# Third graph layer: the vector engine's steps of the last passage put behind the pair product, and fewer, wider writes on GpSimd

## What is computed

```python
log_ij = _logmap(x[:, None, :], x[None, :, :], c)      # every pair of nodes
agg = jnp.einsum('ij,ijc->ic', adj / deg, log_ij)
transformed = agg @ weight + bias
return _expmap(origin, transformed, c)                 # tanh of the row's length, times the row
...
# the layer after it (index 3)
support = layernorm_relu(x) @ weight3                  # then a rank-weighted sum over the neighbours
```

## Time and profile before

| | us |
|---|---|
| three runs | 1113.17, 1117.30, 1118.21 |
| median | 1117.3 |
| the profiled execution | 1117.34 |
| its span | 1115.6 |
| third layer, unit 0's pair product to the last one's | 580.1 to 1003.9 |
| the last passage's steps in it | 814.4 to 982 |

### The profile page before, as it was taken

One profiled execution on the slowest core, in us unless ns is written; L12 is line 12 of the kernel. 1 busy time (PEld: TensorE's weight loads), 2 busy tenths in 40 slices (PEclk: granted clock), 3 DMA queues, 4 the chain that ended last, 5 costly groups with the idle time before them and its releaser, 6 DMA issues.

```text
span 1115.6 us, 14859 instructions
## 1 busy us (share of the span) xinstructions
PE 1038.4 (93%) x5404; PEld 457.0 (41%) x5404; DVE 865.2 (78%) x1011; ACT 757.6 (68%) x803; POOL 272.7 (24%) x145
## 2 busy tenths in 40 slices
PE   4899999999669999999998998999999998989998
PEld 1233333336643333333333443444544454436544
DVE  6999989996476666688668977877779887778781
ACT  2454554543355666686688889888888888777782
POOL 3179300000010000004005364444343433330010
PEclk9999999998879999999999999999999999989999
DMA  7999999991008888787764444555545545446451
GB/s 264 409 390 351 355 355 317 356 363 56 1 4 298 279 287 283 260 277 272 256 198 140 145 132 158 181 176 170 183 151 189 161 160 189 132 145 223 133 180 39
DMA packets 98438, 240.42 MB, mean 215 GB/s; under 512 B 16449, under 2 KB 47169, under 8 KB 81985
## 3 DMA queue, kind: packets, MB, share of 16 engines
q1 hardware_dynamic: 89152, 222.72, 58.1%
q10 hardware_dynamic: 9216, 16.78, 3.9%
HBM read 221.65 MB, written 17.83 MB: 215 GB/s over the span
## 4 chain that ended last, share of the span: by engine, by line
PE 49%; issue 22%; POOL 13%; DVE 9%; ACT 5%; DMA 1%; SPq 1%; POOLq 0%; DVEq 0%; ACTq 0%
PE PS L555 35%; POOL ring L533 10%; PE PS L701 5%; PE PS L702 5%; POOL H L533 2%; DVE TB L1445 1%; DMA ring<-in_adj_t 1%; ACT work L1105 1%; PE PS L567 1%; DVE work L1894 1%; PE PS L589 1%; PE PS L579 1%; DVE work L1440 1%; PE PS L831 1%; ACT work L1008 1%
## 5 line engine op out<-in xcount | busy, mean ns | idle before, releaser
L1571 DVE TENSOR_TENSOR work<-work,ring 128x1024 f32<-128x1024 f32 x128 | 151.1, 1223 | 78.7 <-ACT work L1105 78.7
L1042 ACT ACTIVATE work<-PS 128x1024 uint8<-128x1024 f32 x128 | 124.1, 1020 | 120.3 <-PE PS L555 120.3
L1105 ACT ACTIVATE work<-PS,att_sc 128x1024 f32<-128x1024 f32 x128 | 147.5, 1201 | 80.3 <-PE PS L702 72.7
L555 PE MATMUL PS<-ring,work 128*65 128x256 f32 (+1 forms) x612 | 194.1, 466 | 2.2 <-DVE work L1922 1.2
L533 POOL TENSOR_TENSOR ring<-work,ring 128x1024 f32<-128x1024 f32 (+1 forms) x57 | 134.0, 2352 | 245.7 <-DVE work L1894 245.6
L555 PE MATMUL PS<-work 128*64 128x512 f32 (+3 forms) x800 | 153.6, 524 | 1.1 <-ACT work L1168 1.0
L1888 DVE SCALAR_TENSOR_TENSOR work<-PS,work 128x1024 f32<-128x1024 f32 x72 | 85.8, 1192 | 56.4 <-PE PS L555 49.9
L555 PEld LDWEIGHTS PS<-ring,work 128*65 128x65 f32 x612 | 83.5, 140 | 91.8 <-issue 66.9
L701 PE MATMUL PS<-work 128*128 128x512 f16 x256 | 98.8, 386 | 4.2 <-DVE work L1394 2.5
L1174 ACT ACTIVATE work<-work 128x1024 f32<-128x1024 f32 x72 | 74.2, 1031 | 37.2 <-DVE work L1882 37.2
L702 PE MATMUL PS<-work 128*128 128x512 f16 x256 | 98.2, 383 | 0.0
(11 more groups left out here) (248 smaller groups left out, 1488.9 us busy)
## 6 DMA issues: line engine op xcount, KB each, us to landing
ring<-in_adj_t SPq DMA_DIRECT2D x96, 1024.0 KB, 5.2
ring<-in_adj_t SPq DMA_DIRECT2D x107, 512.0 KB, 3.8
work<-in_adj_t SPq DMA_DIRECT2D x32, 1024.0 KB, 7.6
codes<-work ACTq DMA_DIRECT2D x64, 256.0 KB, 6.6
ring<-codes SPq DMA_DIRECT2D x64, 256.0 KB, 3.8
H<-in_adj_t SPq DMA_DIRECT2D x25, 512.0 KB, 3.8
X<-in_x SPq DMA_DIRECT2D x2, 512.0 KB, 5.2
out_x<-X SPq DMA_DIRECT2D x1, 512.0 KB, 3.8
```

The lines of the kernel that those rows point to most:

```text
L555: return mm(out_ap, lhsT, rhs, start=starts, stop=True, skip_group_check=True)
L1042: nc.scalar.activation(made[:, k, u * UNIT:(u + 1) * UNIT], PS[:, (4 + 2 * u) * BANK:(6 + 2 * u) * BANK], ACT.Relu).then_inc(sem("codes_ma ...
L1105: nc.scalar.activation(att[:, u, :], PS[:, (4 + 2 * u) * BANK:(6 + 2 * u) * BANK], ACT.Sigmoid, bias=att_sc[:, 2:3], scale=att_sc[:, 1:2]) ...
L1571: V.tensor_tensor(prob[:, m % 4, :], att[:, u, :], ring[:, s % RING, u * UNIT:(u + 1) * UNIT], ALU.mult)\
```

## The change

Three things are altered.

1. In DVE's loop `last_passage2(n)` and the early `near2_out` stand behind `pair2(n)`, not ahead of it.
2. The steps stand in other turns, in smaller parts, up to turn 70. PE's and ACT's tables follow: `to_last(0)` and `weighted_last(0)` move from 51 and 52 to 57 and 58, `to_tangent(1)` and `weighted(1)` from 57 and 58 to 59 and 60.
3. In POOL's `aux_nodes` two writes of 128 x 48 become one of 128 x 96, three times per call.

```diff
@@ POOL, aux_nodes
                 for k in range(3):
                     link(nc.gpsimd.tensor_copy(ALn[:, :, 3 * k:3 * k + 3], ...))
-                    for d in range(2):
-                        link(nc.gpsimd.tensor_copy(ARn[:, :, d, k:9:3], tpart[k][:, :].unsqueeze(2).broadcast_to([P, TG, 3])))
+                    link(nc.gpsimd.tensor_copy(ARn[:, :, :, k:9:3], tpart[k][:, :].unsqueeze(2).unsqueeze(3).broadcast_to([P, TG, 2, 3])))
@@ DVE, last_passage2 (turn: steps)
-40: tangent_dot(0), tangent_scale(0)
+39: tangent_dot(0)   40: tangent_scale(0)
 41: tangent_own(0), tangent_sum(0)   44: length(0)
-45: tanh_num(0, 0, 5)
+45: tanh_num(0, 0, 2)   46: tanh_num(0, 2, 5)
-46: length_root(0)   47: tanh_den(0), tanh_end(0)
+47: length_root(0)   48: tanh_den(0)   49: tanh_end(0)
-48: step_v(0), step_x(0)   49: mean3(0), centre3(0)
+50: step_v(0)   51: step_x(0)   52: mean3(0)   53: centre3(0)
-50: spread3(0)   51: feats3(0)   53: rest_a(0)   54: rest_b(0)
+54: spread3(0)   56: feats3(0)   59: rest_a(0)   60: rest_b(0)
-56: tangent_dot(1), tangent_scale(1)   57: tangent_own(1), tangent_sum(1)
+55: tangent_dot(1)   57: tangent_scale(1)   58: tangent_own(1), tangent_sum(1)
-60: length(1)   61: tanh_num(1, 0, 5)   62: length_root(1)
+62: length(1)   63: tanh_num(1, 0, 5)   64: length_root(1)
-63: tanh_den(1), tanh_end(1)   66: step_v(1), step_x(1)
+65: tanh_den(1)   66: tanh_end(1)   67: step_v(1)   68: step_x(1)
-67: mean3(1), centre3(1)
+69: mean3(1)   70: centre3(1)
@@ DVE, the loop over units
                 second_half2(n)
-                last_passage2(n)
-                if n - 2 in EARLY:
-                    near2_out(n - 2)
                 if n == NU - 1:
                     power(0)
                 pair2(n)
+                if n - 2 in EARLY:
+                    near2_out(n - 2)
+                last_passage2(n)
```

More of the change, by code:

```diff
@@ L79 @@
 COPIES = (2, 4, 7)
-VISITS = {38: ("agg2_copied", 2), 41: ("turned_out", 1), 42: ("z_out", 1), 51: ("turned_out", 2), 52: ("z_out", 2),
-          54: ("agg2_copied", 4), 57: ("turned_out", 3), 58: ("z_out", 3)}
+VISITS = {38: ("agg2_copied", 2), 42: ("turned_out", 1), 43: ("z_out", 1), 54: ("agg2_copied", 4),
+          57: ("turned_out", 2), 58: ("z_out", 2), 59: ("turned_out", 3), 60: ("z_out", 3)}
 CAUGHT = 16
@@ L875, in last_passage2 @@
                     nodes2(0)
-                if n == 41:
+                if n == 42:
                     to_tangent(0)
-                if n == 42:
+                if n == 43:
                     weighted(0)
[L880 to L883, removed]
                 if n == 54:
@@ L886, in last_passage2 @@
                 if n == 57:
+                    to_last(0)
+                if n == 58:
+                    weighted_last(0)
+                if n == 59:
                     to_tangent(1)
-                if n == 58:
+                if n == 60:
                     weighted(1)
@@ L1228, in last_passage2 @@
                     nodes2_out(0)
-                if n == 42:
+                if n == 43:
                     turned_out(0, 1)
-                if n == 43:
+                if n == 44:
                     z_out(0, 1)
@@ L1235, in last_passage2 @@
                     root_part("v_root", "v_norm2", 0, 0)
-                if n == 50:
+                if n == 54:
                     ln_square(0)
-                if n == 51:
+                if n == 55:
                     root_part("ln_sd", "ln_var", 3 * G, 0)
-                if n == 52:
+                    nodes2_out(1)
+                if n == 58:
                     turned_out(0, 2)
-                if n == 53:
+                if n == 59:
                     z_out(0, 2, W_SCALE)
                     part_a(0, 2)
-                if n == 54:
+                if n == 60:
+                    turned_out(1, 3)
                     part_b(0)
[L1247 to L1251, removed]
+                if n == 61:
                     z_out(1, 3)
-                if n == 60:
+                if n == 62:
                     v_square(1, 3)
-                if n == 61:
+                if n == 63:
                     root_part("v_root", "v_norm2", 1, 1)
@@ L1816, in last_passage2 @@
                     coefficients()
+                if n == 39:
+                    tangent_dot(0)
                 if n == 40:
-                    tangent_dot(0)
                     tangent_scale(0)
@@ L1825, in last_passage2 @@
                 if n == 45:
-                    tanh_num(0, 0, 5)
+                    tanh_num(0, 0, 2)
                 if n == 46:
+                    tanh_num(0, 2, 5)
+                if n == 47:
                     length_root(0)
-                if n == 47:
+                if n == 48:
                     tanh_den(0)
+                if n == 49:
                     tanh_end(0)
-                if n == 48:
+                if n == 50:
                     step_v(0)
+                if n == 51:
                     step_x(0)
-                if n == 49:
+                if n == 52:
                     mean3(0)
+                if n == 53:
                     centre3(0)
-                if n == 50:
+                if n == 54:
                     spread3(0)
-                if n == 51:
+                if n == 55:
+                    tangent_dot(1)
+                if n == 56:
                     feats3(0)
[L1842 to L1847, removed]
+                if n == 57:
                     tangent_scale(1)
-                if n == 57:
+                if n == 58:
                     tangent_own(1)
                     tangent_sum(1)
+                if n == 59:
+                    rest_a(0)
                 if n == 60:
+                    rest_b(0)
+                if n == 62:
                     length(1)
-                if n == 61:
+                if n == 63:
                     tanh_num(1, 0, 5)
-                if n == 62:
+                if n == 64:
                     length_root(1)
-                if n == 63:
+                if n == 65:
                     tanh_den(1)
+                if n == 66:
                     tanh_end(1)
-                if n == 66:
+                if n == 67:
                     step_v(1)
+                if n == 68:
                     step_x(1)
-                if n == 67:
+                if n == 69:
                     mean3(1)
+                if n == 70:
                     centre3(1)
```

## The result

The changed kernel takes 1138.8 us (median of four runs, 1136.4 to 1141.4), the kernel before 1116.2 us (1113.2 to 1118.2). The ratio is 1.020, with a 95% interval of 1.018 to 1.023: slower by 22.5 us, where 1135 us was forecast.

What follows compares the result with a forecast made beforehand. PE was taken to set the period, 5.86 us per pair product, with DVE having 1.35 us of slack. Terms 11.6 + 2.5 + 3.3 + 1.8 - 1.0 = +18.2 us on 1117.34 gave 1135 us, range 1110 to 1146.

Steps and rivals of the forecast that it cites:

- The mechanism: Behind the pair product, a step's second DVE operation waits for POOL's near product, 2.3 us; single-operation steps cost nothing.
- the unseen order: A DVE operation with two SBUF operands coming second to POOL: bounds 0 and 2.37 us, taken as 2.3.
- Rivals 1, 2 and 3: Only one-operand operations wait (1126, 0.13); no step waits for POOL (1110 to 1112); POOL waits each time; last two together 0.25.
- Rival 2: No step waits for POOL, each part fits DVE's slack: faster, 1110 to 1112 us; 0.25 together with the third rival.
- 58 to 62: Turns 58 to 61 and the transposes of turn 62: these come later despite moved visits, lower clock stays; +2.5 us.
- the middle: Turns 40 to 57: PE loses the DVE lag beyond 1.55 us, 12.7 us, less 1.1 of small waits; net +11.6.
- the slack: DVE's waits for PE ahead of far2_out and sum2 in a turn without steps: 1.35 us per turn.
- Rival 4: Turns 45 to 49: idle times of some 1.9 us lower the clock, up to 6 us more, 1141; chance within the forecast's 0.62.
- 62 to 67: Turns 62 to 67: lag from steps costs PE, less 1.2 us of small waits; about +3.3 us; turn 68's wait remains.
- near_out(69): After turn 71: near2_out(69) behind power(0) and the pair product delays PE's sum; +1.8 us, 0 at least.
- `near2_out(17)`: Moved behind the pair product it costs nothing, since PE waits for turn 20's pair product behind it anyway.
- POOL's writes: At aux_nodes(1): merged writes shorten PE's wait of 1.28 us; -1.0 us, bounds 0 and -1.28.

Runs made afterwards that it cites:

- ten steps behind: The changed kernel with its steps ahead of the pair product again, except ten one-operation steps left behind it: 1110.9 us, ratio 0.994 to the kernel before.
- `near_out` alone: The kernel before with only the early near2_out(17) and near2_out(69) moved behind power(0) and the pair product: 1120.2 us, ratio 1.0025.

## Why the prediction was right

**The mechanism** was that a step's second operation waits for POOL's near product. It is shown twice: in the rows (2.35 us for 0.17, in all 19 steps of several operations) and by moving POOL's start alone, which takes back 18 to 20 us. The value taken for the unseen order, 2.3 us, was measured at 2.2 of excess. The Trainium skill (SBUF — State Buffer, "Who interferes with whom") states both orders of this exclusion; the trace now agrees for both. The same section of the Trainium skill says that a reduction never contends on this chip; the trace agrees (0.68 us at 847.98). At 607.90 POOL's row starts 0.10 us before that of `rest2`, right at the end of POOL's near product; that POOL came second there is inferred from its standing still. Rivals 1, 2 and 3 fall: two-operand operations wait, steps of several operations do too, and DVE isn't let through first. Rival 2's time, 1110 to 1112, would not have come even without the conflict: that kernel (the changed one, POOL waiting) has a ratio of 1.004.

That the total came so close, 1135 for 1138.8, is partly luck: the turns 58 to 62 were put 2 us too high, the middle 1.7 and the end 3.3 us too low.

**The middle, 39 to 58:** +11.6 forecast, +13.3 measured. The size was nearly right, the place where PE feels it was not. I followed only the transposes' wait for the pair product. PE's larger waits are for `far2_out` and `near2_out`, which I had left out of the slack. The sum came out because DVE's period sets the time, whichever wait shows it: from the pair product of turn 44 to that of turn 50 DVE is busy for 43.6 of 44.5 us, where it was for 34.2 of 35.8 before. The pair products there are 6.8 to 8.1 us apart. The sum had no term for two things. One is PE's waits for ACT's copies at the visits (4.9 us, 1.1 before); these are in turns 43 and 58, where the turn behind a visit waits for its copy; `to_tangent(0)` and `weighted(0)` had moved too, from turns 41 and 42 to 42 and 43. The other is the clock. PE's idle time grew by 10.3 us where the forecast had 11.6, and the clock added some 3: it was half for 3.4 us twice, behind a wait of 2.26 us in turn 43 and one of 2.55 us in turn 46.

```profile
835.12 1.32 PE L830 MATMUL PS<-ident,work 128*128 128x128 f32 x8 [2.26 <-ACT TA L1007]
...
836.23 5.09 PE L554 MATMUL PS<-ring,work 128*65 128x512 f32 x12
...
859.12 5.32 PE L554 MATMUL PS<-H,work 128*65 128x512 f32 x12 [2.55 <-DVE work L1929]
```

Rival 4 had the clock, but over five turns in a row with small waits (45 to 49); from 863.1 us on it stayed up through the rest of them.

**58 to 62:** +2.5 forecast, +0.5 measured. This is the term that was sized wrongly. Followed, the transposes of turn 62 came 4.4 us later and the lower clock stayed. In the profile PE's waits there are 1.46 and 0.80 us, where it had 2.71 before, and the transposes of pair 61 take 1.09 us: the clock stayed up (1.00, before 0.93). That the moved visits filled PE better than I gave them credit for is my reading; no run separates it.

**62 to 67:** +3.3 forecast, +3.8 measured, but not from the waits forecast alone. The largest is 2.50 us, ahead of the scores of unit 67 (999.68), for `sum2` (1895). The wait of 2.94 us ahead of the transposes in turn 68, which was to remain, is 1.10 us now, and the stage 67 to 71 is 0.7 us shorter. The two stages together: +3.3 forecast, +3.1 measured. The sum left out turns 65 and 69, whose units are half as wide; their second operations wait 1.1 and 0.6 us.

**near_out(69):** the wait was right to 0.1 us (+1.8), the term was too small. The lower clock behind this wait adds 1.5 us, which the sum had at nothing; alone the edit costs 2.9 us (1.5 to 4.2). In the profile of the kernel after, a further 1.6 us go between turn 71 and the transposes at 1074: the clock is half for 3.4 us, from 1037.2 on. That is no consequence of the late `near2_out`. The profiles of six kernels with it ahead have the same stretch, the kernel with the wider writes alone among them, and there the stage behind unit 71 takes 113.9 us where the profile of the kernel before has 112.3. `near2_out(17)` cost nothing, as forecast.

**POOL's writes:** PE's wait fell from 1.28 to 0.54 us, 0.74 for a forecast 1.0. The third write is 0.92 us and the last operation of the call 1.24, since both still meet DVE's operations. From unit 0 to unit 39 the profiles of the seven kernels with the wider writes take 226.4 to 227.7 us, mean 226.9, those of the five without 227.5 to 228.4, mean 227.9: the 1.0 us of the forecast.

**Where the gain sits:** the forecast said that a better place could win little in the middle and most of it in turns 62 and 68. With the new turns and the steps ahead, 39 to 58 gains 2.6 us. 58 to 71 gains 5.3 us in the profiles, but 1.5 of it come back behind unit 71, and other profiles with the old order there have 71.3 to 75.8 us. The gain of the whole, by the ratio, is 3.8 us (2.0 to 5.6), within the 7.8 at most that rival 2 counted.

## What to carry to other kernels

Before small work is put into an engine's gap, ask what its neighbour does in that gap: DVE's slack behind the pair product was real, but it was POOL's time at the port. What reads one operand from PSUM can run there: `sum2` at 792.20 takes its 1.22 us beside POOL. Where DVE and POOL alternate, put chains of dependent DVE operations in POOL's idle time; a single operation can go right behind the one that starts POOL, since it gets ahead. When a producer moves within its turn, move the consumers' visits with it, and leave whatever others wait for (`near2_out`, `far2_out`) ahead of the filler.

## What was unexpected of the hardware

- A DVE operation of eight elements per partition waits as long as one of 512: 2.35 us (1747), and 2.73 us in all for 128x512 (1739). What it pays is POOL's operation, not its own size: behind half-wide near products of 1.27 us (turns 65 and 69) a second operation takes 1.26 and 0.75 us.
- POOL, once it waits, gets in between two DVE operations that depend on each other, though the gap is only 0.03 us; in none of the steps did a second operation get ahead of it.
- The length of a single wait of PE doesn't decide whether the clock falls. In the kernel after it fell behind waits of 2.26, 2.50, 2.55 and 3.14 us, but not behind 2.68 us in turn 58 (eight transposes take 1.06 us and the sums behind them 3.61). With ten steps behind it fell behind 1.72 us. And the wait of 2.94 us ahead of the transposes of pair 67, behind which the clock fell in the kernel before (1.97 us for eight), left it up in `near_out` alone, which has the same instructions from turn 20 up to there:

```profile
981.92 1.09 PE L831 MATMUL PS<-ident,work 128*128 128x128 f32 x8 [2.94 <-DVE work L1894]
```

What makes the difference isn't settled here.
